# Half 0's output tiles in two single products, in two successive steps, in place of one pair

## The chip, the cores and the metric

One core of one Trainium2 chip runs one launch. The metric is the device time of that launch in microseconds (us). Before the change the median of three runs is 1953.3 us (1953.26 to 1953.86).

TensorE (PE in the profile) multiplies and leaves its results in PSUM, which has eight banks of 512 fp32 columns for each of 128 partitions. PEld is TensorE's weight load. ScalarE (ACT) takes the exponentials, VectorE (DVE) does arithmetic on SBUF and PSUM, GpSimd (POOL) a few additions, and SyncE (SP) issues most transfers. Each engine works through its own program in order, and engines meet only at semaphores.

## The reference

Input x is 4096 rows of 256. A latent attention with 16 heads of width 16 is followed by a residual and a layer norm, then a linear layer on integers with a residual and a second layer norm. What matters here:

```python
attn = softmax(einsum('bhqd,bhkd->bhqk', query, key) / scale)
out  = einsum('bhqk,bhkd->bhqd', attn, value)      # (1, 16, 4096, 16)
out  = out.transpose(0, 2, 1, 3).reshape(b, s, 256)
x    = _layernorm(x + out @ Wo_w + Wo_b)
x    = _layernorm(x + ffn(x))
```

The change concerns the product `out @ Wo_w` for the first 2048 rows: 16 output tiles of 128 rows by 256 columns. The contraction has 256 terms, so each tile is the sum of two products of 128 terms. Everything here is fp32.

## The kernel before, in words

The queries are cut in two halves of 2048 rows. There are 32 rounds t (half, head), the first 16 for half 0. A round holds scores for 32 key tiles kt by four query chunks j of 512 columns; a (kt, j) pair is a block. Scores stand in PSUM with keys on the partitions. For three key tiles of a round (15, 30, 31; in round 0 only 15) VectorE takes the exponentials, for all others ScalarE.

ScalarE's part is cut in 1860 groups of two blocks, 58 per round, and PE's program is a loop over as many steps s. At step s it
- waits for the exponentials of group s (`a.exp`) and computes the scores of group s + 3 into the two banks that group s has freed (six banks, three groups of two);
- computes VectorE's score blocks whose turn in `BLOCK_STEP` it is (`block`, about 12 per round), each into one bank (6 or 7), after VectorE has read the block before (`b_bits`);
- computes an output tile of half 0, if s is in `PROJECT_STEP` (`project_first`, tiles n = 0 to 15, steps 1006 to 1295);
- multiplies exponentials by values (`values`), four 128x512 products side by side, in 32 of a round's 58 steps. A step without them is called bare below.

The two score blocks of a group usually lie in different halves of PE's rows (`low = 64 * (kt // UPPER)`); in the last two groups of a round they lie in the same half.

VectorE goes through cycles c. A cycle is one of its key tiles: four times it turns a score block into bits (L911) and does one step of the polynomial of the cycle before on 2048 columns (L931 or L935); then, for 16 cycles from `PROJECT_CYCLE` = 51 on, `add_first` (L966) waits for tile n and adds it to Y; then two operations split the bits (L919, L921). Tile n's product stands in the same bank as VectorE's score blocks. Hence its two ties: the tile waits until the four blocks of its cycle are read (`b_bits`), and the first block of the next cycle waits until the tile is added (`p_added`, L650).

`BLOCK_STEP` gives the steps. Tile 4's cycle has its last block in step 1079, tile 7's in step 1138; the next cycles begin in steps 1084 and 1141.

Of the kernel before, what the change touches and what calls it, by code (L numbers as in the profile page):

```python
# [7 lines left out]
D = 256  # L8
# [9 lines left out]
TH = HALF // 128  # L18
# [4 lines left out]
QB = HALF // CH  # L23
# [14 lines left out]
def by_vector(t):  # L38

    return BY_VECTOR if t else FIRST_BY_VECTOR  # L40
# [45 lines left out]
def make_block_steps():  # L86

    steps = []
    for t in range(NT):
        first = TURN[t] + BEHIND if t else 0  # L90
        last = TURN[t + 1] - BEFORE if t + 1 < NT else STEPS_ALL - 20
        n = FIRST_BLOCKS if t == 0 else len(BY_VECTOR) * QB
        n = min(n, QB * CYCLES - len(steps))
        for k in range(n):
            s = first + (last - first) * k // (n - 1)
            s += s % SLOTS not in BLOCK_PHASES and k < n - 1
            steps.append(s)
    return steps


BLOCK_STEP = make_block_steps()
# [5 lines left out]
def value_bank(t):  # L107

    return BANKS[(t + 1) % 2]


def block_bank(n):
    return BANKS[sum(n > of for of in COPY_AFTER) % 2]
# [35 lines left out]


PROJECT_CYCLE = next(c for c in range(CYCLES) if BLOCK_STEP[QB * c + QB - 1] >= HEAD_STEP[TH + 1])
PROJECT_STEP = {min(BLOCK_STEP[QB * (PROJECT_CYCLE + n) + QB - 1] + 3, BLOCK_STEP[QB * (PROJECT_CYCLE + n + 1)] - 1): n for n in range(TH)}
STATS_BLOCK = QB * (PROJECT_CYCLE + TH)
NORM_BLOCK = STATS_BLOCK + TH + 12

# [1 line left out]
def project_bank(n):  # L157
    return block_bank(QB * (PROJECT_CYCLE + n) + QB - 1)
# [58 lines left out]
def make_vector_steps():  # L217
    steps = []
    for c in range(HALF_CH):
        steps += [(name, c, n) for name in ("add", "high") for n in "kq"]  # L220
        steps += [("square", c, n) for n in "kq"] + [("low", c, n) for n in "kq"]
    for n in "kq":
        steps += [(name, c, n) for c in range(HALF_CH, NCH) for name in ("add", "high", "square", "low")]
    return steps


STEP = {p: n + 1 for n, p in enumerate(make_vector_steps())}
assert len(PROJECT_STEP) == TH and NORM_BLOCK + TH + 8 < QB * CYCLES
KR = 6 * HD
# [41 lines left out]
def build(nc, xT_d, x_d, w_d, bias_d, rows_d, tab_d, sel_d, ident_d, w8_d, out_d,  # L271
# [11 lines left out]
    with ctx:  # L283
# [3 lines left out]
        def sem(name):  # L287
            return ctx.enter_context(nc.semaphore(name))
# [100 lines left out]
        def ring(at, n=1):  # L389

            if at < RING_A:
                return arena[:, at * CH:(at + n) * CH]
            return pool_a[:, (RING_B + at - RING_A) * CH:(RING_B + at - RING_A + n) * CH]
# [30 lines left out]
        def heads_out(half, k, at, n, rows=slice(0, 128)):  # L424

            if half == 0:
                return ctkv[rows, k * HALF + at:k * HALF + at + n]
            return (pool_a[:, 5 * CH:5 * CH + HALF], bits)[k][rows, at:at + n]
# [3 lines left out]
        def bank(b, n=1):  # L432
            return PS[:, b * CH:(b + n) * CH]
# [105 lines left out]
        p_proj = sem("first_tiles_projected")  # L539
# [85 lines left out]
        def attention_tensor(pe, a, behind_first):  # L625
            def score_block(out, par, kt, j):
                low = 64 * (kt // UPPER)
                at = kt % UPPER * 128
                return nc.tensor.matmul(out, Kst[par][low:low + HK + 1, at:at + 128],  # L629
                                        Qst[par][low:low + HK + 1, j * CH:(j + 1) * CH], start=True, stop=True)  # L630

            def scores(g):
                t, blocks = GROUPS[g]
                if g == HEAD_STEP[t]:
                    pe.wait_ge(a.stack[t % 2], STACK_INC * (t // 2 + 1))
                for k, (kt, j) in enumerate(blocks):
                    last = score_block(bank(g % SLOTS * SLOT + k), t % 2, kt, j)
                last.then_inc(a.qk, 1)

            def block(n):  # L640
                c, j = divmod(n, QB)
                t, kt = TILES[c]
                if n == 0:
                    pe.wait_ge(s_shift, 2)
                    pe.wait_ge(s_range, 2)
                if j == 0 and kt == by_vector(t)[0]:
                    pe.wait_ge(a.stack[t % 2], STACK_INC * (t // 2 + 1))
                if j == 0 and PROJECT_CYCLE < c <= PROJECT_CYCLE + TH:

                    pe.wait_ge(p_added, c - PROJECT_CYCLE)  # L650
                if n - 1 in COPY_AFTER:

                    pe.wait_ge(a.norm, NORM0 + NSTEP * COPY_AFTER[n - 1] + 1)
                if n:
                    pe.wait_ge(b_bits, n)
                score_block(bank(block_bank(n)), t % 2, kt, j).then_inc(b_qk, 1)

            def values(t, kt):
                first, last_kt = VALUE_ORDER[KT * t][1], VALUE_ORDER[KT * t + KT - 1][1]
                if kt == first:  # L660

                    pe.wait_ge(a.vh[t % 2], 16 * (t // 2 + 1))
                    if t == 0:
                        pe.wait_ge(s_v0, 3)
                        pe.wait_ge(s_sums, 1)
                    if t:

                        pe.wait_ge(b_bits, COPY_BLOCK[t - 1] + 1)
                    if t == 2:
                        pe.wait_ge(s_ones, ONES_ALL)  # L670
                vector = kt in by_vector(t)
                if vector:
                    c = TILES.index((t, kt))
                    pe.wait_ge(b_exp, c + 1)
                for j in range(QB):
                    at = None if vector else PLACE[t, kt, j]
                    moving = poly[c % 2][:, j * CH:(j + 1) * CH] if vector else ring(at)
                    last = nc.tensor.matmul(bank(value_bank(t))[32 * j:32 * j + 32, :],  # L678
                                            Vh[t % 2][:, kt, :], moving, start=kt == first, stop=kt == last_kt)
                last.then_inc(a.pv, 1)  # L680

            def project_first(n):
                if n == 0:
                    pe.wait_ge(a.heads[0], 16 * 2)
                    pe.wait_ge(a.yb, KT)

                pe.wait_ge(b_bits, QB * (PROJECT_CYCLE + n + 1))
                project_tile(n, bank(project_bank(n))[:, 0:D]).then_inc(p_proj, 1)

            bias_out()  # L690
            for g in range(SLOTS):
                scores(g)
            behind_first()
            for s in range(STEPS_ALL + 1):
                if s < STEPS_ALL:
                    pe.wait_ge(a.exp, s + 1)
                if s + SLOTS < STEPS_ALL:
                    scores(s + SLOTS)
                for n, at in enumerate(BLOCK_STEP):
                    if at == s:  # L700
                        block(n)
                if s in PROJECT_STEP:
                    project_first(PROJECT_STEP[s])
                for t, kt in VALUES[s]:
                    values(t, kt)

        def bias_out():

            for k in range(2):
                last = nc.tensor.matmul(PS[:, OT * CH:OT * CH + D], bv_wide[:, k, :],  # L710
                                        w[:, W_O + k * D:W_O + (k + 1) * D], start=k == 0, stop=k == 1)
            last.then_inc(s_bo, 1)

        def project_tile(t, out, cs=(0, 1), starts=True, stops=True):


            for c in cs:
                last = nc.tensor.matmul(out, heads_out(t // TH, c, t % TH * 128, 128),  # L718
                                        w[:, W_O + c * D:W_O + (c + 1) * D], start=c == 0 and starts, stop=c == 1 and stops)
            return last  # L720
# [390 lines left out]
        def _(pe):  # L1111
# [81 lines left out]
            pe.wait_ge(s_rows_in, 64)  # L1193

            attention_tensor(pe, fast, lambda: lengths("q", 1, Q_LENGTH_BANKS[1]))


# [651 lines left out]
```

## Time and profile before

| | |
|---|---|
| median of three runs | 1953.3 us |
| profiled execution, its own time | 1949.75 us |
| span of its trace | 1947.9 us |
| PE busy | 1858.2 us (95%) |
| ACT busy | 1802.0 us (93%) |
| DVE busy | 1575.4 us (81%) |
| steps (ScalarE's groups) | 1860 |
| stretch with the 16 output tiles | about 1070 to 1350 us |
| granted TensorE clock in it | 1.00 |

The profiled execution is 3.5 us below the median of the timed runs. Times of rows count from the span's start. "L718 PE" is a matmul issued by line 718. A value in brackets is idle time of the engine before the row, with what ended it. A matmul of fp32 is recorded as two, so an output tile of two products is x4 and one of `values` is x8. Records of successive matmuls overlap, so PE's pace is read from start to start.

### The profile page before, as it was taken

Reading aid. Unit: us, or ns where it says so; the run is one execution under the profiler, and the core shown is the slowest. Engines: PE = TensorE matmul, PEld = TensorE weight load, DVE = VectorE, ACT = ScalarE, POOL = GpSimd, SP = SyncE. Lnnn points to the kernel's source line nnn. Section 1 sums busy time; section 2 is a strip of 40 time slices with the busy share of each in tenths; the row PEclk is TensorE's granted clock in tenths of the full one; section 3 lists DMA queues with packets and bytes.
Section 4 is the critical chain, followed back from the end, with each engine's and each line's share of the span. In section 5 each row is a group of like instructions: output and inputs, shape, how many; then the busy total and the mean of one; then the engine's idle time right before and its main releaser. Section 6 shows DMA issues by size and latency. Waiting matters only on the chain.

```text
span 1947.9 us, 31445 instructions
## 1 busy us (share of the span) xinstructions
PE 1858.2 (95%) x12996; PEld 452.8 (23%) x12996; DVE 1575.4 (81%) x1499; ACT 1802.0 (93%) x2022; POOL 162.5 (8%) x132
## 2 busy tenths in 40 slices
PE   8969999999999999999999999999999999999975
PEld 3331222122222222222222222222222112222234
DVE  4745988888888888888888888888988898888467
ACT  4349999999999999999999999999999999999945
POOL 5643700000000000000000000000000300000011
PEclk9989999999999999999999999999999999999987
DMA  4434111111011111111121011111121011111002
GB/s 140 151 110 167 26 25 25 26 26 25 20 19 21 18 26 26 26 25 25 25 64 30 14 18 20 25 25 26 26 47 25 17 20 18 22 26 25 1 24 87
DMA packets 161527, 73.67 MB, mean 38 GB/s; under 512 B 129984, under 2 KB 146624, under 8 KB 160896
## 3 DMA queue, kind: packets, MB, share of 16 engines
q1 hardware_dynamic: 158432, 67.12, 14.9%
q10 hardware_dynamic: 2944, 4.47, 0.8%
q8 instruction: 104, 1.70, 0.4%
q14 instruction: 47, 0.39, 0.1%
HBM read 49.39 MB, written 20.84 MB: 36 GB/s over the span
## 4 chain that ended last, share of the span: by engine, by line
ACT 61%; PE 22%; issue 10%; DVE 5%; DMA 1%; POOL 0%; SPq 0%; ACTq 0%; DVEq 0%; POOLq 0%
ACT arena L875 60%; PE PS L678 9%; PE PS L629 6%; PE PS L1152 4%; PE PS L718 1%; DVE arena L935 1%; PE PS L1301 1%; DMA arena<-tables_dram 1%; DVE bn L806 1%; DVE arena L931 0%; DMA arena<-xT_dram 0%; DVE arena L911 0%; DMA w<-weights_dram 0%; DVE absmax L1743 0%; DVE arena L1777 0%
## 5 line engine op out<-in xcount | busy, mean ns | idle before, releaser
L875 ACT ACTIVATE arena<-PS 128x1024 f32<-128x1024 f32 x1860 | 1708.1, 1336 | 16.2 <-PE PS L629 15.8
L678 PE MATMUL PS<-arena,Vh 128*32 128x512 f32 x8192 | 1092.9, 606 | 6.2 <-DVE arena L935 4.2
L629 PE MATMUL PS<-Qst,Kst 49*128 49x512 f16 x4096 | 728.6, 385 | 25.2 <-ACT arena L875 4.3
L935 DVE SCALAR_TENSOR_TENSOR arena<-arena 128x2048 f32<-128x2048 f32 x282 | 646.2, 2291 | 0.1
L911 DVE TENSOR_SCALAR arena<-PS 128x512 int32<-128x512 f32 x376 | 259.4, 690 | 252.4 <-PE PS L629 249.1
L629 PEld LDWEIGHTS PS<-Qst,Kst 49*128 49x128 f16 x4096 | 190.1, 93 | 1047.4 <-ACT arena L875 1020.6
L678 PEld LDWEIGHTS PS<-arena,Vh 128*32 128x32 f32 x8192 | 161.4, 108 | 314.9 <-issue 298.4
L931 DVE SCALAR_TENSOR_TENSOR arena<-arena 128x2048 f32<-128x2048 f32 x94 | 216.4, 2302 | 0.0
L919 DVE TENSOR_SCALAR arena<-arena 128x2048 int32<-128x2048 int32 x94 | 115.6, 1230 | 7.7 <-DVE arena L935 0.5
L921 DVE TENSOR_SCALAR arena<-arena 128x2048 int32<-128x2048 int32 x94 | 116.8, 1242 | 0.0
L1469 POOL TENSOR_SCALAR nmr<-mv 128x16 f32<-128x16 f32 x1 | 0.3, 263 | 1195.2 <-DVE mv L1633 1195.2
L1152 PE MATMUL PS<-arena,w 128*128 128x512 f32 x176 | 83.7, 622 | 11.0 <-DMA w<-weights_dram 6.2
L1349 ACT ACTIVATE arena<-PS,bias 128x512 f32<-128x512 f32 x56 | 37.3, 686 | 47.9 <-PE PS L1152 36.3
L848 POOL TENSOR_TENSOR arena<-arena,rows 128x256 f32<-128x256 f32 x32 | 51.3, 1639 | 45.3 <-DMA arena<-x_dram 45.3
L1543 DVE TENSOR_TENSOR arena<-arena 128x512 f32<-128x512 f32 x16 | 18.1, 1143 | 36.6 <-POOL arena L1452 29.0
L1152 PEld LDWEIGHTS PS<-arena,w 128*128 128x128 f32 x176 | 34.6, 199 | 56.0 <-issue 46.7
L852 POOL TENSOR_TENSOR arena<-arena,rows 128x256 f32<-128x256 f32 x16 | 11.1, 733 | 332.8 <-ACT arena L838 332.8
L1449 POOL TENSOR_TENSOR arena<-arena 32x512 f32<-32x512 f32 x16 | 23.6, 1473 | 51.6 <-DMA arena<-arena 40.0
L852 POOL TENSOR_TENSOR ctkv<-arena,rows 128x256 f32<-128x256 f32 x16 | 17.5, 1130 | 114.9 <-DVE arena L833 114.9
L1450 POOL TENSOR_TENSOR arena<-arena 32x512 f32<-32x512 f32 x16 | 26.2, 1639 | 0.0
L1554 DVE TENSOR_TENSOR parts_or_sums<-arena,parts_or_sums 128x1024 f16<-128x1024 f32 x16 | 25.9, 1641 | 0.0
L885 DVE COPY parts_or_sums<-PS 128x512 f32<-128x512 f32 x32 | 21.8, 683 | 4.0 <-PE PS L678 4.0
(118 smaller groups left out, 481.4 us busy)
## 6 DMA issues: line engine op xcount, KB each, us to landing
Kst<-k_halves SPq DMA_DIRECT2D x64, 128.0 KB
Qst<-q_halves SPq DMA_DIRECT2D x64, 128.0 KB
Vh<-head_values SPq DMA_DIRECT2D x30, 256.0 KB, 5.5
k_halves<-parts_or_sums SPq DMA_DIRECT2D x16, 256.0 KB, 2.6
q_halves<-parts_or_sums SPq DMA_DIRECT2D x16, 256.0 KB, 2.8
Kst<-k_halves SPq DMA_DIRECT2D x64, 64.0 KB
Qst<-q_halves SPq DMA_DIRECT2D x64, 64.0 KB
head_values<-arena SPq DMA_DIRECT2D x1, 4096.0 KB, 18.2
```

The source lines that it names most:

```text
L629: return nc.tensor.matmul(out, Kst[par][low:low + HK + 1, at:at + 128], Qst[par][low:low + HK + 1, j * CH:(j + 1) * CH], start=True, stop= ...
L678: last = nc.tensor.matmul(bank(value_bank(t))[32 * j:32 * j + 32, :], Vh[t % 2][:, kt, :], moving, start=kt == first, stop=kt == last_kt)
L848: nc.gpsimd.tensor_tensor(Y[:, t, :], Y[:, t, :], bo, ALU.add).then_inc(s, 1)
L852: nc.gpsimd.tensor_tensor(Z[half][:, t, :], Y[:, TH * half + t, :], fb, ALU.add).then_inc(s, 1)
L875: nc.scalar.activation(ring(at, k), bank(g % SLOTS * SLOT, k), ACT.Exp, scale=EXP_SCALE).then_inc(a.exp, 1)
L911: nc.vector.tensor_scalar(bits[:, j * CH:(j + 1) * CH].bitcast(int32), bank(block_bank(n)), LOWEST, TO_BITS, ALU.max, ALU.mult).then_inc(b ...
L919: nc.vector.tensor_scalar(mantissa.bitcast(int32), bits.bitcast(int32), 0x007FFFFF, 0x3F800000, ALU.bitwise_and, ALU.bitwise_or).then_inc( ...
L921: nc.vector.tensor_scalar(power.bitcast(int32), bits.bitcast(int32), 0x7F800000, 0x40000000, ALU.bitwise_and, ALU.bitwise_xor).then_inc(b_ ...
L931: nc.vector.scalar_tensor_tensor(out=t, in0=mantissa, scalar=POLY[3], in1=mantissa, op0=ALU.add, op1=ALU.mult).then_inc(b_poly, 1)
L935: last = nc.vector.scalar_tensor_tensor(out=t, in0=t, scalar=POLY[3 - j], in1=power if j == 3 else mantissa, op0=ALU.add, op1=ALU.mult)
L1152: last = nc.tensor.matmul(bank(b), l, r, start=k == 0, stop=k == len(lhsT) - 1)
L1349: nc.scalar.activation(dst, bank(b), ACT.Identity, bias=at, scale=1.0 if e in (DKV, DQ_) else K_SCALE if n == "k" else Q_SCALE).then_inc(s ...
```

## The change

Tile n is computed in two steps. Its first product (rows 0 to 127 of the heads' output) is computed where the tile was, or one step earlier where the next cycle's first block would otherwise come too soon; the second product in the step behind, after that step's scores and blocks and ahead of its values.

```diff
-PROJECT_STEP = {min(BLOCK_STEP[QB * (PROJECT_CYCLE + n) + QB - 1] + 3, BLOCK_STEP[QB * (PROJECT_CYCLE + n + 1)] - 1): n for n in range(TH)}
+PROJECT_STEP = {min(BLOCK_STEP[QB * (PROJECT_CYCLE + n) + QB - 1] + 3, BLOCK_STEP[QB * (PROJECT_CYCLE + n + 1)] - 2): n for n in range(TH)}
...
                 pe.wait_ge(b_bits, QB * (PROJECT_CYCLE + n + 1))
-                project_tile(n, bank(project_bank(n))[:, 0:D]).then_inc(p_proj, 1)
+                project_tile(n, bank(project_bank(n))[:, 0:D], (0,))
+
+            def project_first_rest(n):
+                project_tile(n, bank(project_bank(n))[:, 0:D], (1,)).then_inc(p_proj, 1)
...
                 if s in PROJECT_STEP:
                     project_first(PROJECT_STEP[s])
+                if s - 1 in PROJECT_STEP:
+                    project_first_rest(PROJECT_STEP[s - 1])
                 for t, kt in VALUES[s]:
                     values(t, kt)
```

The first product moves one step forward in tiles 0, 1, 7, 8, 9 and 10 (1006, 1024, 1140, 1159, 1180, 1198 become 1005, 1023, 1139, 1158, 1179, 1197) and keeps its step in the other ten, whose second product goes one step back. The number of matmuls is the same, and no other engine's program changes.

PE's program at tile 4, steps 1082 to 1084, before. L629 is a score product, L678 one of `values`, L718 an output product; "a_exps" is the wait for ScalarE's group, and each such row begins a step.

```order
3175 L629 MATMUL PS<-Qst,Kst 128x512 [waits a_exps]
3176 L629 MATMUL PS<-Qst,Kst 128x512
3177 L718 MATMUL PS<-w,ctkv 128x256 [waits block_bits]
3178 L718 MATMUL PS<-w,ctkv 128x256
3179 L678 MATMUL PS<-arena,Vh 32x512 x4
3180 L629 MATMUL PS<-Qst,Kst 128x512 [waits a_exps]
3181 L629 MATMUL PS<-Qst,Kst 128x512
3182 L629 MATMUL PS<-Qst,Kst 128x512 [waits a_exps]
3183 L629 MATMUL PS<-Qst,Kst 128x512
3184 L629 MATMUL PS<-Qst,Kst 128x512 [waits block_bits,first_residuals_added]
```

The same place after the change, where the output product's line is L723:

```order
3175 L629 MATMUL PS<-Qst,Kst 128x512 [waits a_exps]
3176 L629 MATMUL PS<-Qst,Kst 128x512
3177 L723 MATMUL PS<-w,ctkv 128x256 [waits block_bits]
3178 L678 MATMUL PS<-arena,Vh 32x512 x4
3179 L629 MATMUL PS<-Qst,Kst 128x512 [waits a_exps]
3180 L629 MATMUL PS<-Qst,Kst 128x512
3181 L723 MATMUL PS<-w,ctkv 128x256
3182 L629 MATMUL PS<-Qst,Kst 128x512 [waits a_exps]
3183 L629 MATMUL PS<-Qst,Kst 128x512
3184 L629 MATMUL PS<-Qst,Kst 128x512 [waits block_bits,first_residuals_added]
```

The second product has moved behind the values of step 1082 and the scores of step 1083. Only the two scores of step 1084 now stand between it and the block that waits for the tile's addition.

PE's program at tile 7, steps 1138 to 1140, before:

```order
3338 L629 MATMUL PS<-Qst,Kst 128x512 [waits a_exps]
3339 L629 MATMUL PS<-Qst,Kst 128x512
3340 L629 MATMUL PS<-Qst,Kst 128x512 [waits block_bits]
3341 L629 MATMUL PS<-Qst,Kst 128x512 [waits a_exps]
3342 L629 MATMUL PS<-Qst,Kst 128x512
3343 L678 MATMUL PS<-arena,Vh 32x512 x4
3344 L629 MATMUL PS<-Qst,Kst 128x512 [waits a_exps]
3345 L629 MATMUL PS<-Qst,Kst 128x512
3346 L718 MATMUL PS<-w,ctkv 128x256 [waits block_bits]
3347 L718 MATMUL PS<-w,ctkv 128x256
```

And after it:

```order
3338 L629 MATMUL PS<-Qst,Kst 128x512 [waits a_exps]
3339 L629 MATMUL PS<-Qst,Kst 128x512
3340 L629 MATMUL PS<-Qst,Kst 128x512 [waits block_bits]
3341 L629 MATMUL PS<-Qst,Kst 128x512 [waits a_exps]
3342 L629 MATMUL PS<-Qst,Kst 128x512
3343 L723 MATMUL PS<-w,ctkv 128x256 [waits block_bits]
3344 L678 MATMUL PS<-arena,Vh 32x512 x4
3345 L629 MATMUL PS<-Qst,Kst 128x512 [waits a_exps]
3346 L629 MATMUL PS<-Qst,Kst 128x512
3347 L723 MATMUL PS<-w,ctkv 128x256
```

The first product has moved ahead of the values of step 1139. It waits for VectorE's read of the score block in row 3340, and only the two scores of step 1139 now stand between the two.

## Rows read from the trace of the kernel before

**Rows 1.** Windows of the span: us, busy us of each engine, clock, DMA share, GB/s
```profile
800.00:1000.00 200.00, 197.53 (x1450) 41.65 (x1443) 169.12 (x137) 200.00 (x219) 0.00 (x0) 1.00 0.13 21
1070.00:1350.00 280.00, 278.59 (x2010) 65.21 (x2006) 231.76 (x203) 271.23 (x295) 0.00 (x0) 1.00 0.12 22
```
**Rows 2.** Timeline of ACT: start, us, engine, line, operation, [idle before]; tiles 1 to 4, later
```profile
1091.51 16.61 ACT L875 ACTIVATE arena<-PS 128x1024 f32<-128x1024 f32 x18 [0.52 <-PE PS L629]
1108.89 20.31 ACT L875 ACTIVATE arena<-PS 128x1024 f32<-128x1024 f32 x22 [0.78 <-PE PS L629]
1129.55 16.61 ACT L875 ACTIVATE arena<-PS 128x1024 f32<-128x1024 f32 x18 [0.35 <-PE PS L629]
1146.67 16.61 ACT L875 ACTIVATE arena<-PS 128x1024 f32<-128x1024 f32 x18 [0.52 <-PE PS L629]
...
1350.67 201.77 ACT L875 ACTIVATE arena<-PS 128x1024 f32<-128x1024 f32 x220 [0.35 <-PE PS L629]
```
**Rows 3.** Chain that ended last, 1085 to 1104 us, around tile 1: start, us, what
```profile
1084.33 1.16 ACT arena L875
1085.49 0.05 issue
1085.54 0.60 PE PS L629 x3
1086.14 0.99 PE PS L678 x8
1087.14 0.63 PE PS L629 x4
1087.77 0.99 PE PS L678 x8
1088.76 0.32 PE PS L629 x2
1089.08 1.06 PE PS L718 x4
1090.14 0.99 PE PS L678 x8
...
1101.31 1.00 PE PS L678 x8
```
**Rows 4.** Timeline of PE, tile 0, from windows of growing start
```profile
1071.29 0.60 PE L629 MATMUL PS<-Qst,Kst 49*128 49x512 f16 x4
1071.83 1.13 PE L718 MATMUL PS<-w,ctkv 128*128 128x256 f32 x4
1072.15 0.81 PE L718 MATMUL PS<-w,ctkv 128*128 128x256 f32 x3
1072.37 0.59 PE L718 MATMUL PS<-w,ctkv 128*128 128x256 f32 x2
1072.89 1.06 PE L678 MATMUL PS<-arena,Vh 128*32 128x512 f32 x8
```
**Rows 5.** Timeline of PE and of DVE, tile 1
```profile
1089.01 1.13 PE L718 MATMUL PS<-w,ctkv 128*128 128x256 f32 x4
...
1086.18 0.69 DVE L911 TENSOR_SCALAR arena<-PS 128x512 int32<-128x512 f32 x1 [0.88 <-PE PS L629]
1086.79 2.28 DVE L935 SCALAR_TENSOR_TENSOR arena<-arena 128x2048 f32<-128x2048 f32 x1
1090.18 0.42 DVE L966 TENSOR_TENSOR arena<-PS,arena 128x256 f32<-128x256 f32 x1 [1.11 <-PE PS L718]
```
**Rows 6.** Timeline of all engines, tile 7, from step 1138's scores on
```profile
1197.20 0.91 PE L629 MATMUL PS<-Qst,Kst 49*128 49x512 f16 x5
1197.84 0.69 DVE L911 TENSOR_SCALAR arena<-PS 128x512 int32<-128x512 f32 x1 [2.20 <-PE PS L629]
1198.03 1.06 PE L678 MATMUL PS<-arena,Vh 128*32 128x512 f32 x8
```
**Rows 7.** Timeline of PE, steps 1043 and 1044, with a round's last two groups
```profile
1108.19 1.03 PE L629 MATMUL PS<-Qst,Kst 49*128 49x512 f16 x4
1109.16 1.06 PE L678 MATMUL PS<-arena,Vh 128*32 128x512 f32 x8
```
**Rows 8.** Waits by engine, 1060 to 1350 us: in total, times, longest
```profile
DVE arena L911 <- PE PS L629: 32.2, 34, 2.5
DVE arena L966 <- PE PS L718: 15.4, 15, 1.3
```
**Rows 9.** Instructions of L718: engine, op, count: ns min/median/max, first and last start
```profile
L718 PE MATMUL PS<-w,ctkv x64: 379/379/483, 1071.8 to 1348.6; 128*128 128x256 f32 x64
```

## The prediction

> **What bounds the kernel now.** I read the page's windows first, then ScalarE's timeline, then the chain of waits around one tile. Before the tiles ScalarE is busy for the whole of 200 us; in the stretch with the 16 tiles it is busy 271.2 of 280 us, and PE 278.6 [rows 1]. So ScalarE sets the pace everywhere but there, where it stalls once or twice per tile for scores [rows 2]. Its undisturbed pace is 201.77 / 220 = 0.917 us per group. From 1091.51 to 1146.67 us it does 18 + 22 + 18 = 58 groups, which should take 53.19 us and take 55.16: 1.97 us lost for three tiles, 0.66 each, some 10.5 us for all 16. That is all that a better placing of this work could win back.
>
> A tile costs PE 1.06 us (1071.83 to 1072.89) [rows 4], and 0.66 of it comes out as a stall. The rest is cover: PE runs three groups ahead and may be late by that much. The reader is to see in the chain what happens around tile 1 [rows 3]: from 1085.54 us on, 3.5 us ahead of the tile, until 1102 us, some 12 us behind it, no piece of the chain is a wait for ScalarE. PE goes from matmul to matmul and catches up slowly, since a step with values and a bare one take 1.3 + 0.23 us against 1.83 for two groups. In that run it is of no account in which of two neighbouring steps a piece of work is done. The groups of the next steps are late by all that stands ahead of them, and a half that leaves the first step stands in the second.
>
> **The change part by part.** Moving half of a tile by a step earns nothing, by the above: the stall is cut in two and its sum stays, as far as PE's work is the same. It isn't quite.
>
> (a) Each product by itself. Within a tile the matmuls start 0.32 (1071.83 to 1072.15), 0.22 (to 1072.37) and again 0.22 us apart, and the values begin 0.30 us after the last: 1.06 in all [rows 4]. The first interval is 0.10 longer since nothing hides the first weight load; the last is 0.08 to 0.09 longer since the next kind of matmul waits for the one before it to leave. The tile now pays each toll once. In two parts it pays each twice: 2 x (0.32 + 0.31) = 1.26 us, 0.20 more. For 16 tiles: 3.2 us.
>
> (b) A bare step that now holds a product. Scores of two bare steps in a row take 0.54 for both (1071.29 to 1071.83) [rows 4], and one pair ahead of something else 0.32 [rows 3], so a pair followed by scores takes 0.22, and the second toll, 0.10, is new in a step that was bare. In tiles 0 and 9 the first product gets such a step: 0.2 us. In tiles 2, 4, 5, 8, 11, 13 and 14 the second does, another 0.7; but there the pair of steps that follows the stall (0.23 + 1.52) has 0.08 us of room in 1.83, which takes it. I enter 0.2 and keep 0.9 for the upper end.
>
> (c) Tile 7 waits for VectorE. Its product now comes one step after the last score block instead of two. VectorE starts reading that block at 1197.84 and takes 0.69, to 1198.53 [rows 6]; with 0.05 for the signal (the "issue" between an end and a start [rows 3]) that is 1198.58. PE has the place free at 1198.03, where the values now start. It waits 0.55 us, and behind it are the values and all scores. In tile 1, another of those moved forward, the block is read at 1086.18 + 0.69 = 1086.87 [rows 5], and the place is at 1087.7 [rows 3]: no wait.
>
> (d) The next block waits for the addition. In tile 1 the addition starts at 1090.18, 1.17 us behind the tile's start at 1089.01 [rows 5], so 0.41 behind the start of its last matmul, which comes at 0.76. A second product by itself has its last matmul 0.32 behind its start: addition at 0.73, 0.42 long, signal 0.05, released at 1.20. PE is through with the product after 0.63, and with the next step's scores 0.23 later: it waits 0.34. This holds for tiles 4 and 13, where no values stand between and the block is in the very next step. In tiles 5 and 14 those scores are the end of a round and share PE's rows; there two pairs take 0.97 (1108.19 to the values at 1109.16) and the first 0.44 [rows 7], which leaves 0.15. Tile 8 is alike, but has that wait before the change too (1.06 + 0.44 against 1.17 + 0.42 + 0.05). Sum: 0.7 + 0.3 = 1.0 us. In the other tiles values or another step stand between.
>
> (e) VectorE gets ten tiles later. Where values stand between the products (tile 4: 0.63 + 1.00 + 0.32 + 0.73 = 2.68 instead of 1.17) it waits 1.5 us longer. It idles 32.2 + 15.4 us in this stretch [rows 8], 3.0 per tile, so the delay fits into waits that it would have had for score blocks. Entered at nothing; without that cover it costs up to 1.5 us in seven tiles.
>
> PE's waits in (c) and (d) fall in its unbroken run and come out in full. Sum: 3.2 + 0.2 + 0.55 + 1.0 = 4.95, say 5.0 us. The profiled execution has 1949.75 us and would have 1954.7; the median of the runs lies 3.5 above it, and 1953.3 + 5.0 = 1958.3 us. Bounds: without any toll (a) and (b) fall away and the waits in (d) grow by 0.1 each, to 1.4: + 2.0. With all of (b): + 5.7; with the stalls' own scatter (0.35 to 0.78 us [rows 2]) I take + 7.
>
> The row shows 0.32 us to a tile's second matmul and 0.22 afterwards [rows 4], hence a weight load in the open. The Trainium skill (TensorE: Matmul & The Clock Gate, "Architectural detail: the array is 16× 32×32, not 1× 128×128") states that PE's queue is a partial reorder window that pulls weight loads ahead of matmuls in flight. By that rule the second product's weights would be loaded under the scores and the split would cost no load. The same page ("The mechanism") limits it to loads into other row groups, and the weights here fill all 128 rows; this case's row agrees with the limit. By the first rule the sum would be near 3, by the second 5.
>
> **The rivals.**
> - *No toll.* The second product's load hides under the scores and the pieces close up. For it: inside a tile the loads do hide (0.22). Against it: the first of a tile doesn't. + 2.0 us, 1955.3. It stays within what counts as no change up to a toll of (3.9 - 2.0) / 16 = 0.12 us per tile.
> - *The split smooths the stall.* Half a tile fits into the cover of 0.4 us (0.53 of 1.06), PE recovers before the second half, and most of the stall goes: per tile 2 x (0.53 - 0.4) instead of 0.66, a gain of 0.4 x 16 = 6.4 less (c) and (d): 1948.5. It needs a wait for ScalarE between the halves. The chain shows none in the steps around the tile, neither ahead nor behind [rows 3].
> - *VectorE becomes the bound.* Additions up to 1.5 us later delay the split of bits and with it PE's next score blocks; PE waits in seven tiles: up to 7 x 1.5 = 10.5 on top, 1968.8. It decides where VectorE's spare time per tile is below 1.5 us. Against it: 3.0 us [rows 8], which however isn't evenly spread.
> - *Nothing happens*, since the moves and tolls fall in waits of PE. Speaks against it that PE is busy 278.6 of 280 us [rows 1].
>
> **How the numbers follow.** What tells a change from none here is about 0.2%, 3.9 us. Forecast (+ 3.5 to + 7): 0.66. No toll, or hardly any, with nothing happening: 0.23. Smoothing: 0.07. VectorE: 0.04. The forecast lies only 1.1 us above the bound for "slower", so I move 0.04 of it to "same". Faster 0.07, same 0.27, slower 0.66. The range 1954.8 to 1961.0 takes in the no-toll case and + 7 and leaves out smoothing, the VectorE case and a rest.
>
> **What would show it.** In the changed kernel's profile the output product of half 0 has 64 matmuls of which 32, not 16, are of the long first kind (483 instead of 379 ns [rows 9]), and each product takes 0.63 us start to start. ScalarE has more and shorter stalls, whose sum grows from 10.5 to about 15.5 us. PE waits half a microsecond for VectorE in tile 7 and 0.3 for the addition in tiles 4 and 13. VectorE's wait for the tiles grows from 15.4 to about 28 us, its wait for score blocks shrinks. The forecast is wrong if ScalarE's stalls shrink in sum, or if the second product takes less than 0.55 us.

## The result

| | before | after |
|---|---|---|
| median of 9 runs each | 1953.26 us | 1958.42 us |
| ratio of the two | 1 | 1.0029, 95% interval 1.0019 to 1.0039 |
| profiled execution | 1949.75 us | 1958.04 us |
| span of its trace | 1947.9 us | 1956.2 us |

The changed kernel is slower by 5.2 us, and by the interval of the ratio 3.7 to 7.6 us. Forecast were 5.0. Of the executions in the table of the experiments two were slow ones (2295 us in e4, 3412 us in the kernel before beside e1 to e4); the ratios leave them out, the medians don't.

The two profiled executions lie further apart, by 8.3 us, and only a part of that is the change. ScalarE's first group starts at 142.2 us before and 144.2 after, 2.0 us that pass ahead of the attention (in the traces of the experiments it starts at 143.5 to 147.8 us). The stretch of the tiles gives 5.4 us. Some 0.9 us are a longer stall near group 1520, where TensorE ran at half its clock after a pause (last section); that isn't the change's either, since e4 and e6, which split nothing, have it too. So the readings here are taken from the stretch of the tiles. Where two kernels have the same program there (before and e9), it repeats to less than 0.1 us.

The windows of the changed kernel that answer to [rows 1]:

```profile
800.00:1000.00 200.00, 197.50 (x1450) 41.52 (x1442) 168.68 (x138) 200.00 (x219) 0.00 (x0) 1.00 0.13 22
1070.00:1355.00 285.00, 282.88 (x2006) 63.22 (x2004) 231.44 (x202) 272.29 (x295) 0.00 (x0) 1.00 0.13 23
```

Away from the tiles nothing moved. With them, ScalarE does as many groups (x295) in 5 us more.

ScalarE's timeline of the changed kernel, the rows that answer to [rows 2] and the first and last of the stretch:

```profile
1067.11 8.67 ACT L880 ACTIVATE arena<-PS 128x1024 f32<-128x1024 f32 x9
1076.58 16.61 ACT L880 ACTIVATE arena<-PS 128x1024 f32<-128x1024 f32 x18 [0.80 <-PE PS L629]
1093.90 16.61 ACT L880 ACTIVATE arena<-PS 128x1024 f32<-128x1024 f32 x18 [0.71 <-PE PS L629]
1110.86 2.13 ACT L880 ACTIVATE arena<-PS 128x1024 f32<-128x1024 f32 x2 [0.35 <-PE PS L629]
1113.29 18.45 ACT L880 ACTIVATE arena<-PS 128x1024 f32<-128x1024 f32 x20 [0.29 <-PE PS L629]
...
1188.85 15.69 ACT L880 ACTIVATE arena<-PS 128x1024 f32<-128x1024 f32 x17 [0.58 <-PE PS L629]
1204.77 1.02 ACT L880 ACTIVATE arena<-PS 128x1024 f32<-128x1024 f32 x1 [0.23 <-PE PS L629]
1206.72 16.61 ACT L880 ACTIVATE arena<-PS 128x1024 f32<-128x1024 f32 x18 [0.92 <-PE PS L629]
...
1357.97 4.69 ACT L880 ACTIVATE arena<-PS 128x1024 f32<-128x1024 f32 x5 [0.57 <-PE PS L629]
```

This gives the measure used from here on, called the stall sum: the time between the starts of groups 1003 and 1302 less 299 x 0.917 us, groups counted from 0. The first row above begins with group 1001 and the last with group 1300; group 1003 starts at 1068.92 and group 1302 at 1359.80, and 290.88 - 274.18 = 16.7 us. In the kernel before it is 11.3. (The prediction had 10.5, from three tiles; tile 8 alone, whose next block waits for the addition already, costs 1.2.) Tile by tile: tile 1 costs 1093.90 - 1076.58 - 18 x 0.917 = 0.81 us, where it cost 1091.51 - 1074.38 - 16.51 = 0.62. Tile 2's one stall [rows 2] has become two, with two groups between: this is the smoothing, and its sum is 0.2 us larger. Tile 7 has grown from 0.6 to 1.36 us (1188.85 to 1206.72, 18 groups).

PE's timeline at tile 4 (steps 1082 to 1084), and VectorE's:

```profile
1146.94 0.70 PE L723 MATMUL PS<-w,ctkv 128*128 128x256 f32 x2
1147.57 1.07 PE L678 MATMUL PS<-arena,Vh 128*32 128x512 f32 x8
1148.56 0.39 PE L629 MATMUL PS<-Qst,Kst 49*128 49x512 f16 x2
1148.88 0.70 PE L723 MATMUL PS<-w,ctkv 128*128 128x256 f32 x2
1149.52 0.39 PE L629 MATMUL PS<-Qst,Kst 49*128 49x512 f16 x2
1150.10 0.39 PE L629 MATMUL PS<-Qst,Kst 49*128 49x512 f16 x1 [0.20 <-DVE arena L971]
1150.42 1.06 PE L678 MATMUL PS<-arena,Vh 128*32 128x512 f32 x8
```

```profile
1149.62 0.42 DVE L971 TENSOR_TENSOR arena<-PS,arena 128x256 f32<-128x256 f32 x1 [2.62 <-PE PS L723]
```

Each product takes 0.63 us from its start to the next kind of matmul (1146.94 to 1147.57, and 0.64 from 1148.88 to 1149.52), and so do the 30 others of the trace. The block of step 1084 would follow its scores 0.23 us after 1149.52 and starts at 1150.10, 0.35 later, because the addition ran from 1149.62 to 1150.04. The same place in the kernel before, from the values of step 1082 to those of step 1084:

```profile
1145.24 1.06 PE L678 MATMUL PS<-arena,Vh 128*32 128x512 f32 x8
1146.99 1.06 PE L678 MATMUL PS<-arena,Vh 128*32 128x512 f32 x8
```

It took 1.75 us there and takes 2.85 now (1147.57 to 1150.42). These 1.10 us are the second product (0.63), 0.10 for the pair of scores ahead of it (0.32 from 1148.56 to 1148.88, where a pair ahead of scores takes 0.22) and the wait. Ahead of the values the tile's 1.06 us have become 0.63, so PE is 0.67 us later in all. Tile 4's stall has grown by just that: the second toll of (b) comes out in full here.

The timeline at tile 7, where the first product waits for VectorE's read:

```profile
1201.97 0.69 DVE L916 TENSOR_SCALAR arena<-PS 128x512 int32<-128x512 f32 x1 [2.20 <-PE PS L629]
1202.71 0.70 PE L723 MATMUL PS<-w,ctkv 128*128 128x256 f32 x2 [0.48 <-DVE arena L916]
```

The waits of PE's weight loads and of VectorE from 1060 to 1355 us (the latter answer to [rows 8]):

```profile
PEld PS L629 <- DVE arena L971: 2.4, 5, 0.5
PEld PS L723 <- DVE arena L916: 0.8, 1, 0.8
```

```profile
DVE arena L971 <- PE PS L723: 27.5, 15, 2.8
DVE arena L916 <- PE PS L629: 24.3, 25, 2.5
```

Five tiles' next blocks now wait for the addition, where tile 8's alone did. VectorE waits 12.1 us more for tiles and 7.9 less for score blocks. The output products' durations, to be held against [rows 9]:

```profile
L723 PE MATMUL PS<-w,ctkv x64: 379/431/483, 1073.5 to 1356.2; 128*128 128x256 f32 x64
```

The median between 379 and 483 ns says that 32 of the 64 matmuls are now of the long first kind.

### The profile page after: what moved, and what is told of

It is laid out like the page before. It is cut to its first block, busy times and chain, and to the rows that moved or that the text cites. A ratio compares the mean times of both kernels' runs of the same rounds, so it can differ in the third digit from the quotient of the medians.

```text
span 1956.2 us, 31445 instructions
## 1 busy us (share of the span) xinstructions
PE 1864.8 (95%) x12996; PEld 452.2 (23%) x12996; DVE 1576.5 (81%) x1499; ACT 1803.1 (92%) x2022; POOL 161.8 (8%) x132
## 4 chain that ended last, share of the span: by engine, by line
ACT 62%; PE 22%; issue 10%; DVE 4%; DMA 2%; POOL 0%; SPq 0%; ACTq 0%; DVEq 0%; POOLq 0%
ACT arena L880 61%; PE PS L678 9%; PE PS L629 6%; PE PS L1157 4%; PE PS L723 2%; DVE arena L940 1%; PE PS L1306 1%; DVE bn L811 1%; DMA arena<-tables_dram 1%; DMA arena<-xT_dram 0%; DMA w<-weights_dram 0%; DVE arena L916 0%; DVE absmax L1748 0%; DVE arena L1782 0%; DVE arena L803 0%
## 5 line engine op out<-in xcount | busy, mean ns | idle before, releaser
L678 PE MATMUL PS<-arena,Vh 128*32 128x512 f32 x8192 | 1094.1, 606 | 5.7 <-DVE arena L940 3.7
L629 PE MATMUL PS<-Qst,Kst 49*128 49x512 f16 x4096 | 731.0, 385 | 25.1 <-ACT arena L880 4.4
L916 DVE TENSOR_SCALAR arena<-PS 128x512 int32<-128x512 f32 x376 | 259.5, 690 | 244.6 <-PE PS L629 241.2
L629 PEld LDWEIGHTS PS<-Qst,Kst 49*128 49x128 f16 x4096 | 190.1, 93 | 1050.7 <-ACT arena L880 1020.2
L678 PEld LDWEIGHTS PS<-arena,Vh 128*32 128x32 f32 x8192 | 161.4, 108 | 315.2 <-issue 299.7
L971 DVE TENSOR_TENSOR arena<-PS,arena 128x256 f32<-128x256 f32 x16 | 6.8, 425 | 29.2 <-PE PS L723 29.2
L1454 POOL TENSOR_TENSOR arena<-arena 32x512 f32<-32x512 f32 x16 | 22.8, 1427 | 54.3 <-DMA arena<-arena 43.3
```

The source lines that it names most:

```text
L916: nc.vector.tensor_scalar(bits[:, j * CH:(j + 1) * CH].bitcast(int32), bank(block_bank(n)), LOWEST, TO_BITS, ALU.max, ALU.mult).then_inc(b ...
```

## The experiments

All ten are variants of one of the two kernels, timed beside the kernel before on their chip. The intervals of the ratios are 1.6 to 3 us wide to either side, so effects of 1 or 2 us are read from the stall sums, of which each comes from one trace.

| kernel | median, before's beside it | ratio, 95% interval | stall sum |
|---|---|---|---|
| before | | | 11.3 |
| the change | 1958.4, 1953.3 | 1.0029 (1.0019 to 1.0039) | 16.7 |
| e1, 11 tiles split | 1955.6, 1953.5 | 1.0009 (1.0000 to 1.0018) | 13.6 |
| e2, the other 5 split | 1955.6, 1953.5 | 1.0011 (1.0002 to 1.0020) | 14.4 |
| e3, whole, first step | 1953.9, 1953.5 | 1.0004 (0.9995 to 1.0013) | 11.7 |
| e4, whole, second step | 1954.4, 1953.5 | 1.0005 (0.9996 to 1.0014) | 12.3 |
| e5, one more product | 1961.9, 1954.0 | 1.0039 (1.0025 to 1.0052) | 18.2 |
| e6, VectorE + 1.3 us | 1953.8, 1954.0 | 0.9999 (0.9990 to 1.0007) | 11.3 |
| e7, VectorE + 2.5 us | 1967.0, 1954.0 | 1.0066 (1.0051 to 1.0081) | 22.8 |
| e8, a cycle apart | 1950.2, 1954.0 | 0.9980 (0.9972 to 0.9989) | 4.4 |
| e9, norms late | 1952.5, 1953.1 | 0.9996 (0.9987 to 1.0004) | 11.3 |
| e10, apart and placed | 1948.5, 1953.1 | 0.9974 (0.9965 to 0.9983) | 3.5 |

In e8 and e10 half of the products lie behind group 1302, so their sums are told below over a longer stretch.

**e1 and e2: the change in two parts.** Tiles that `WHOLE` names are computed whole in their old step.

```diff
+WHOLE = (4, 5, 7, 13, 14)
-... BLOCK_STEP[QB * (PROJECT_CYCLE + n + 1)] - 2): n for n in range(TH)}
+... BLOCK_STEP[QB * (PROJECT_CYCLE + n + 1)] - 2 + (n in WHOLE)): n for n in range(TH)}
...
-                if s - 1 in PROJECT_STEP:
+                if s - 1 in PROJECT_STEP and PROJECT_STEP[s - 1] not in WHOLE:
```

> The change in the 11 tiles where neither product meets a wait for VectorE; tiles 4, 5, 7, 13 and 14 stay whole where they were before the change. What is left is the price of a product by itself: 11 x 0.20 us and 0.10 each in tiles 0 and 9, so 2.3 to 2.4 us above the kernel before, and ScalarE's stalls in the stretch of the tiles (11.3 us before, 16.7 in the changed kernel, counted as the time from group 1003 on less 0.917 us per group) at 13.7. Rival A (a product by itself costs nothing, only the waits do): + 0, stalls 11.3. Rival B (a tile in two steps smooths the stalls, and the waits of the five tiles hid that): below the kernel before, stalls under 11.

The stall sum is 13.6, 2.3 us more than before: the price of the split where no wait is near, 0.21 us per tile. Tile by tile it is 0.30 us in tiles 0 and 9, where the 0.10 of (b) comes on top, and 0.17 to 0.20 in the others. Both rivals fall by the trace, A by 2.3 us, B by its sign; the interval of the times begins at 1.0000 and leaves A barely out.

> The other part of the change: tiles 4, 5, 7, 13 and 14 in two steps, the 11 others whole where they were before. Theory: 5 x 0.20 for products by themselves, 0.55 for tile 7's wait for VectorE's read, 0.34 + 0.34 + 0.15 + 0.15 for blocks that wait for the addition, and some 0.1 for tolls in bare steps: 2.6 us, stalls 14.0; with the first run it adds up to the whole change (5.0). Rival A: the waits alone, grown by 0.1 where the product is shorter, 2.0 us. Rival B: 1.5 us less the gain.

14.4, or 3.1 us more, where 2.6 were expected. The parts add up to the whole (2.3 + 3.1 = 5.4 = 16.7 - 11.3). The missing 0.5 us lies in four of these tiles, 4, 5, 13 and 14; e4 shows why. Rival A (2.0) is off by twice as much, B by its sign again.

**e3 and e4: whole tiles, moved by a step.**

```diff
-... BLOCK_STEP[QB * (PROJECT_CYCLE + n + 1)] - 1): n for n in range(TH)}
+... BLOCK_STEP[QB * (PROJECT_CYCLE + n + 1)] - 2): n for n in range(TH)}
```

and for e4 the same with `PROJECT_STEP = {1 + min(...`.

> No split: whole tiles in the steps where the change puts the first product, so tiles 0, 1, 7, 8, 9 and 10 are one step earlier than before. Theory (in PE's unbroken run the step of a piece of work is of no account): nothing but tile 7's wait for VectorE's read of the last score block, + 0.5 us, stalls 11.8. Rival (the place counts: the change loses because its first products come too early): about + 2 us or more, shared by six tiles.

> No split: whole tiles in the steps where the change puts the second product, so the ten tiles other than 0, 1, 7, 8, 9 and 10 are one step later than before. Theory: the blocks of tiles 4 and 13 wait 0.35 us for the addition, those of 5 and 14 0.15, four bare-step tiles (3, 6, 12, 15) gain 0.1 each: + 0.8 us or less, stalls 12.1 at the most. Rival (second products come too late and take the time): + 3 us or more.

11.7 and 12.3. Six tiles one step early cost 0.4 us. Tile 7 costs 0.55 us more, tiles 0 and 9 some 0.1 each in a bare step, and tile 8 gains 0.36, which the theory had missed: its next block no longer waits for the addition. Tile 7's wait stands in the row:

```profile
1200.71 1.13 PE L718 MATMUL PS<-w,ctkv 128*128 128x256 f32 x4 [0.48 <-DVE arena L911]
```

Ten tiles one step late cost 1.0 us against the 0.8 of the theory. PE at tile 4 in e4, where the whole tile stands in step 1083:

```profile
1146.19 1.07 PE L678 MATMUL PS<-arena,Vh 128*32 128x512 f32 x8
1147.19 0.39 PE L629 MATMUL PS<-Qst,Kst 49*128 49x512 f16 x2
1147.51 1.13 PE L718 MATMUL PS<-w,ctkv 128*128 128x256 f32 x4
1148.58 0.39 PE L629 MATMUL PS<-Qst,Kst 49*128 49x512 f16 x2
1149.16 0.39 PE L629 MATMUL PS<-Qst,Kst 49*128 49x512 f16 x1 [0.20 <-DVE arena L966]
1149.48 1.06 PE L678 MATMUL PS<-arena,Vh 128*32 128x512 f32 x8
```

From values to values these are 3.29 us against 1.75 before. The 1.54 more are, to 0.02, the tile itself (1.06), 0.10 for the scores ahead of it (1147.19 to 1147.51) and 0.36 of wait. The tile's stall has grown by 0.47, where the theory had the wait alone (0.35). In tiles 5 and 14 it has grown by 0.34, against 0.15. So in these four tiles 0.12 and 0.19 us come on top without any split, and the split kernel has the same excess (0.67 for the 0.54 of (a) and (d), and 0.54 for 0.35). In tiles 2 and 11, which also moved to a bare step but have no wait behind them, the stall hasn't changed: there the room of the following steps did take the toll.

Whole tiles moved by a step thus cost 0.4 and 1.0 us, far from the 5.4. Which of two steps holds the work matters only where something waits; the larger part of the cost is that the work is in two pieces.

**e5: added work.** A product whose result the tile's first one overwrites.

```diff
+                nc.tensor.matmul(bank(project_bank(n))[:, 0:D], heads_out(0, 0, n * 128, 128),
+                                 w[:, W_O:W_O + D], start=True, stop=True)
                 project_tile(n, bank(project_bank(n))[:, 0:D]).then_inc(p_proj, 1)
```

> The kernel before with one more product of 128 terms ahead of each tile's two, whose result is overwritten: PE's work grows by two matmuls 0.216 us apart, 0.43 us per tile, and nothing else changes. Theory (PE's work beside a tile comes out in full): 16 x 0.43 = + 6.9 us, stalls 18.2. Rival (a share of added work is still covered, as 0.40 of the tile's 1.06 us is): 16 x 0.43 x 0.62 = + 4.3 us or less.

The rows of tile 0 (PE), then of tiles 0 and 1 (ScalarE):

```profile
1075.39 0.70 PE L688 MATMUL PS<-w,ctkv 128*128 128x256 f32 x2
1076.88 1.06 PE L678 MATMUL PS<-arena,Vh 128*32 128x512 f32 x8
```

```profile
1078.37 16.61 ACT L877 ACTIVATE arena<-PS 128x1024 f32<-128x1024 f32 x18 [0.92 <-PE PS L629]
1095.92 16.61 ACT L877 ACTIVATE arena<-PS 128x1024 f32<-128x1024 f32 x18 [0.95 <-PE PS L629]
```

Three products in one piece take 1.49 us (1075.39 to 1076.88), so one more in a piece costs 0.43, while a piece by itself costs 0.63. Tile 1's stall is 1095.92 - 1078.37 - 16.51 = 1.04 us, 0.42 above the 0.62 of before. Every other tile is up by 0.43 or 0.44 too. The stall sum is 18.2, 6.9 up, as expected: the cover is used up by the tile, and what is added comes out in full.

**e6 and e7: VectorE later.** In the cycles of the tiles the power operation of `split_bits` is done once or twice more behind the addition, with a signal between.

```diff
+            for k in range(1 if 0 <= n - PROJECT_CYCLE < TH else 0):
+                nc.vector.tensor_scalar(power.bitcast(int32), bits.bitcast(int32), 0x7F800000, 0x40000000,
+                                        ALU.bitwise_and, ALU.bitwise_xor).then_inc(x_again, 1)
+                dve.wait_ge(x_again, 1 * (n - PROJECT_CYCLE) + k + 1)
```

> The kernel before with one VectorE operation of 1.2 us more in each of the 16 cycles of the tiles, right behind the addition (the split of bits into powers is done twice), 1.3 us with its signal. Theory (VectorE's later additions cost nothing in the changed kernel): + 0 to + 0.3 us, stalls 11.3 to 11.6. Rival (VectorE became the bound in the changed kernel, where it is up to 1.5 us later in seven tiles): + 2 us or more.

> The same with two operations more, some 2.5 us per cycle. In the rows of before VectorE waits for PE 3.0 us per tile on the average, but the cover ahead of the next cycle's second block is only some 1.2 us in most tiles, so about 1.2 us per tile should come out as PE's waits in 8 to 10 tiles: + 8 to + 13 us. If only the average counted, it would be + 0 to + 2.

With 1.3 us more nothing happens (11.3), with 2.5 us more the sum is 22.8, 11.5 up (13.0 by the medians). PE's waits for VectorE's reads, first in e6, then in e7:

```profile
PEld PS L630 <- DVE arena L912: 2.8, 9, 0.4
```

```profile
PEld PS L630 <- DVE arena L912: 15.5, 11, 1.7
```

So VectorE has room for 1.3 us in each of the 16 cycles, and not for 2.5. The changed kernel makes it up to 2.8 - 1.1 = 1.7 us late, which neither run tries; that this costs nothing is seen in the changed kernel's own trace, where PE has no wait for L916 apart from tile 7's. Of note in e6: PE waits 2.8 us in nine places, and ScalarE loses nothing. These waits come some six steps, 5.9 us, behind the start of a tile, when PE's lateness is past its peak. Together with e5 this says that only what comes ahead of the peak adds to a stall.

**e8 to e10: the two products a cycle apart.** If cover is used once per piece of work, the pieces must lie so far apart that PE catches up between them. In e8 each of 32 cycles takes one product with an addition of its own; statistics, norms and maxima of half 0 follow 16 cycles later.

```diff
+HALVES = 2 * TH
-STATS_BLOCK = QB * (PROJECT_CYCLE + TH)
-NORM_BLOCK = STATS_BLOCK + TH + 12
+STATS_BLOCK = QB * (PROJECT_CYCLE + HALVES)
+NORM_BLOCK = STATS_BLOCK + TH + 3
...
-                project_tile(n, bank(project_bank(n))[:, 0:D]).then_inc(p_proj, 1)
+                project_tile(n // 2, bank(project_bank(n))[:, 0:D], (n % 2,), alone=True).then_inc(p_proj, 1)
...
-            nc.vector.tensor_tensor(Y[:, n, :], bank(project_bank(n))[:, 0:D], Y[:, n, :], ALU.add).then_inc(p_added, 1)
+            nc.vector.tensor_tensor(Y[:, n // 2, :], bank(project_bank(n))[:, 0:D], Y[:, n // 2, :], ALU.add).then_inc(p_added, 1)
```

> The idea of a split with the two products a whole cycle apart (some 18 steps) in place of one step: 32 cycles take one product each, each with an addition of its own, and the statistics and norms of half 0 follow 16 cycles later. Theory: PE catches up between the products, so the cover of about 0.40 us is used twice per tile: stalls per product 0.63 - 0.40 = 0.23 to 0.3 us, 32 of them and a few round ends some 9.5 us instead of 11.3, a gain of 1 to 2 us, unless the later norms show at the end of the attention. Rival (cover is used once, or the additions cost more): no gain or + 3 us.

It is faster than the kernel before by 3.8 us, and the ratio's interval lies below 1. That is more than the 1 to 2 us expected. ScalarE's timeline of e8:

```profile
1109.42 53.52 ACT L876 ACTIVATE arena<-PS 128x1024 f32<-128x1024 f32 x58 [0.35 <-PE PS L630]
1163.29 55.37 ACT L876 ACTIVATE arena<-PS 128x1024 f32<-128x1024 f32 x60 [0.35 <-PE PS L630]
```

Most products leave no gap in these rows, but a row's start shows what was lost: 58 groups from 1109.42 to 1163.29 us take 53.87, 0.69 above 53.19, for three products. Three products are one and a half tiles, which cost 0.98 before (0.66 each). Over all of the attention from group 1003 on the stalls sum up to 9.5 us against 13.1 in the kernel before, 3.6 less. Some of this isn't the products. In the kernel before there is a stall near group 1520 (rows below), which e8 has not, and e8 has one of 1.0 us near group 1788. Hence e9, the kernel before with the late norms alone:

```diff
-NORM_BLOCK = STATS_BLOCK + TH + 12
+NORM_BLOCK = STATS_BLOCK + 4 * TH + TH + 3
```

> The kernel before with VectorE's norms and maxima of half 0 moved to the blocks where the kernel with the products a cycle apart has them (55 blocks later), the tiles as before. That kernel gained 3.8 us: 2.2 us of ScalarE's stalls beside the products, and a stall of 1.3 to 2.3 us around group 1520 that became one of 1.0 us at group 1788. Theory (two separate gains): here the tiles' stalls stay at 11.0 us and the one at group 1520 becomes 1.0 us, so 1.3 to 2.3 us below the kernel before. Rival (all of the gain is the products' distance): no change.

Its stalls over the same stretch are 11.8 us, 1.3 less than before, and the tiles' are unchanged at 11.3. By the traces the gain of e8 is thus 1.3 us of norms and 2.3 us of products. The 1.3 hangs on the execution: the trace of the kernel before is one in which the stall near group 1520 was short (1.9 us from group 1302 to 1640, against 2.5 to 2.8 in e1, e2, e4 and e6, where TensorE's clock fell there). The time of e9 (0.6 us below before, interval across 1) can't tell 1.3 us from none.

> The kernel with the products a cycle apart, 14 of the 32 moved by one or two steps to where the pairs of steps around them have room (a group at the end of a round, whose scores take 0.2 us more, gets its scores first). Theory: stalls beside products 7.4 us instead of 8.7, so 1.4 us less than that kernel and some 5 us below the kernel before. Rival (in PE's unbroken run the step is of no account even here): equal to that kernel.

```diff
+MOVED = {2: 2, 3: 1, 6: 1, 8: -1, 11: 2, 12: 1, 15: 1, 17: -1, 20: 2, 21: 1, 24: 1, 26: -1, 29: 2, 30: 1}
+PROJECT_STEP = {s + MOVED.get(n, 0): n for s, n in PROJECT_STEP.items()}
```

e10 is 4.6 us below the kernel before (1948.5 against 1953.1). Up to group 1640 its stalls are 6.6 us where e8 has 8.5, so the places gave 1.9, where 1.4 were expected. Behind it, around the late norms, this profile has 2.6 us and e8's 1.0: both pause for VectorE there (1.4 us), and in e10 the granted clock is 0.50 from 1799.2 to 1802.5 us, in e8 it stays at 1.00. Whether e10 is faster than e8 the times don't show: they come from two chips, and the intervals of the ratios overlap. Of all kernels run, e10 has the lowest ratio.

## Why the prediction was right

- *What bounds it, and what a better placing could win.* Right. e3 and e4 move whole tiles by a step at 0.4 and 1.0 us, and e5 adds 0.43 us of work per tile and gets 0.43. The stalls to be won were 11.3 us and not 10.5, which changes nothing in the difference.
- *(a) Each product by itself, 0.20 us per tile.* Right: 0.63 us per product in all 32, and 2.3 us for 11 tiles in e1. The size is measured. The reasons given for the two tolls, a load that nothing hides and a kind of matmul that waits for the other to leave, are read into the rows, and no run tests them.
- *(b) Bare steps, 0.2 us entered.* Too small by the 0.4 us that the sum is short of the trace. It holds in tiles 0 and 9 (e1: 2.3 for the 2.4 worked out) and in tiles 2 and 11, where the room of 0.08 us does take the toll. Tile 8, which the prediction lists too, has no new toll: its product stood in that bare step before, and the stall grows by 0.20. The term fails where the next block waits for the addition: tiles 4 and 13 grow by 0.67 us each where 0.20 + 0.34 were counted, tiles 5 and 14 by 0.54 where 0.20 + 0.15 were. In tile 4 the rows show why: toll and wait follow one another in PE's unbroken run, ahead of the peak of its lateness, and 0.20 + 0.10 + 0.37 comes out in full. e4 has the same 0.10 without a split. In tiles 5 and 14 the wait is 0.14 us as forecast and the toll 0.10; the 0.1 us beyond lies at the scores of a round's end, and what it is stays open. The upper end of the range held all of it.
- *(c) Tile 7.* Right: 0.55 us forecast; the stall grows from 0.6 to 1.36, which is 0.55 and the 0.20 of (a).
- *(d) The next block waits for the addition.* Right in place and size: five waits instead of one, 0.35 us at tile 4 for 0.34.
- *(e) VectorE later at no cost.* Right, with little to spare: e6 carries 1.3 us per cycle without loss, e7 shows 11.5 us for 2.5. The delay of the changed kernel, 2.62 - 1.11 = 1.5 us at tile 4, lies between, and comes in seven tiles, not in 16. The mean spare of 3.0 us per tile, by which the prediction argued, would have let e7 through: it was the wrong figure for a right conclusion.
- *The sum.* 5.0 forecast, 5.4 in the trace, 5.2 by the medians. That the median came within 0.1 us of 1958.3 is luck, since the interval of the difference is 3.7 to 7.6 us. The forecast of 1954.7 us for the profiled execution missed by 3.3: it had 2.0 us more ahead of the attention, 0.9 more near group 1520, where the clock fell, and 0.4 with (b). Of the rivals, "no toll" would give 2.0 (e1 alone has 2.3), smoothing a gain; with the pieces in neighbouring steps neither is there. The reordering of weight loads which the Trainium skill describes (TensorE: Matmul & The Clock Gate, "Architectural detail: the array is 16× 32×32, not 1× 128×128") doesn't hide a product's first load here: the second product starts with a matmul of 483 ns, as the first does. The limit to loads into other row groups, which the prediction takes from the same page of the Trainium skill, agrees with that first load only. Inside a product the loads are hidden although the weights fill all 128 rows: the record of the third matmul's load starts at 1072.15 us together with the second matmul, and the third starts at 1072.37 [rows 4]. The measurement decides.
- *Smoothing* fails for the reason given and not in principle: e8 does it with some 18 steps between the pieces, pays for each product by itself as well, and wins.

## What to carry to other kernels

Splitting a burst of work helps only if the engine behind catches up between the pieces; look in the chain of waits how long it runs without a wait for the engine it feeds, here about 12 us, and put the pieces further apart than that. (Tried were one step and some 18, which is 17 us; what lies between wasn't.) Count what each piece pays at its two ends (here 0.10 us at its first matmul and 0.09 at the change of the kind of matmul), and who waits for the last piece. A small cost disappears in the room behind a burst only if nothing waits in between. An average of an engine's idle time says little about what delay it can take: look at the first thing that waits behind the delayed step.

## What the runs showed of the hardware

ScalarE's records hide a part of the pace. The view of one line in the kernel before, from 1074.4 to 1091 us and from 800 to 1000:

```profile
L875 ACT ACTIVATE arena<-PS x18: 1017/1118/1233, 1074.4 to 1089.8; 128x1024 f32<-128x1024 f32 x18
```

```profile
L875 ACT ACTIVATE arena<-PS x219: 1189/1457/1578, 799.4 to 999.0; 128x1024 f32<-128x1024 f32 x110
```

The same operation is 1.02 us long behind a stall and grows to 1.58 in a run without one. In the 18 groups starts are (1089.8 - 1074.4) / 17 = 0.906 us apart, whereas 220 groups take 0.917 each: within a run starts come too close by 0.01 us per group, and durations take up the rest: they grow by (1233 - 1017) / 17 = 13 ns from one group to the next, which puts the ends 0.92 us apart. An idle row on ScalarE therefore reads short (0.52 us at tile 1, whose loss is 0.62), and losses are better counted over many groups.

VectorE slows down beside GpSimd. The timeline of the kernel before near group 1520:

```profile
1543.09 13.60 POOL L852 TENSOR_TENSOR ctkv<-arena,rows 128x256 f32<-128x256 f32 x11 [114.86 <-DVE arena L833]
...
1544.06 1.76 DVE L921 TENSOR_SCALAR arena<-arena 128x2048 int32<-128x2048 int32 x1
...
1546.46 2.79 DVE L931 SCALAR_TENSOR_TENSOR arena<-arena 128x2048 f32<-128x2048 f32 x1
...
1552.14 1.06 PE L678 MATMUL PS<-arena,Vh 128*32 128x512 f32 x8 [2.00 <-issue]
1553.57 1.02 ACT L875 ACTIVATE arena<-PS 128x1024 f32<-128x1024 f32 x1 [1.13 <-PE PS L629]
```

While GpSimd's additions run, two VectorE operations take 0.54 and 0.51 us more than their usual 1.22 and 2.28. Together with the maximum over half 0 (L843, 2.27 us) they make VectorE late, PE stands still for 2.0 us and ScalarE for 1.1. In e9 the norms come later, and GpSimd's additions with them. L921 then takes its usual time near group 1520 and the longer one beside GpSimd:

```profile
1547.34 1.22 DVE L921 TENSOR_SCALAR arena<-arena 128x2048 int32<-128x2048 int32 x1
1790.85 13.00 POOL L852 TENSOR_TENSOR ctkv<-arena,rows 128x256 f32<-128x256 f32 x10 [359.20 <-DVE arena L833]
1798.09 1.75 DVE L921 TENSOR_SCALAR arena<-arena 128x2048 int32<-128x2048 int32 x1
```

So the slowing goes where GpSimd's work goes. VectorE's own norms moved along, and no run took GpSimd away alone, so the cause isn't shown beyond that.

TensorE's clock can fall behind such a pause, and the same pause has either outcome. In the changed kernel PE stands still for 2.00 us as in the kernel before (row at 1552.14 above), but then the granted clock is 0.50, that is 1.2 GHz, where it stayed at 1.00 before. The row of `values` and the window:

```profile
1559.44 1.89 PE L678 MATMUL PS<-arena,Vh 128*32 128x512 f32 x8 [2.00 <-issue]
1559.60:1562.90 3.30, 3.30 (x18) 0.31 (x11) 3.27 (x3) 1.13 (x2) 3.30 (x3) 0.50 0.13 52
```

Four products side by side take 1.89 us instead of 1.06, and ScalarE's stalls from group 1302 to 1640 sum up to 2.8 us instead of 1.9. The traces of e1, e2, e4, e6 and e7 have a clock of 0.50 at this place, those of e3 and e5 don't. A stall of this kind in one trace is therefore no sign of the change.
